# Queries' product ahead of the values' weights, and a last top-k search with keys and counts in PSUM

## The reference, cut to what matters

```python
def _L0_attn_ref(x, w_attn, b_attn, w_proj, b_proj):
    qkv = x @ w_attn + b_attn
    q, k, v = jnp.split(qkv, 3, axis=-1)
    mask = jnp.where(jnp.tril(jnp.ones((Tv, Tv), dtype=jnp.bool_)), 0.0, -10000000000.0)
    attn = jnp.einsum('btc,bsc->bts', q, k) / jnp.sqrt(jnp.float32(Cv)) + mask
    attn = jax.nn.softmax(attn, axis=-1)
    return jnp.einsum('bts,bsc->btc', attn, v) @ w_proj + b_proj

def _L0_ffn_ref(x, w_router, w_block):
    k = max(1, int(L * 0.75))
    _, top_idx = jax.lax.top_k(jnp.einsum('bld,d->bl', x, w_router), k)
    selected = jnp.take_along_axis(x, top_idx[:, :, None], axis=1)
    processed = jax.nn.gelu(jnp.einsum('bkd,de->bke', selected, w_block))
    return x.at[batch_idx, top_idx].set(processed)

x = layernorm(x + _L0_attn_ref(x, ...))
x = layernorm(x + _L0_ffn_ref(x, ...))
```

## Time and profile before

| | |
|---|---|
| device time, median of 3 executions | 1001.97 us |
| lowest, highest | 998.83, 1005.87 us |
| the profiled execution's own time | 998.7 us |
| its span | 997.0 us |
| granted clock, mean over the span | 0.975 |
| busy: PE, weight loads, DVE, ACT, POOL | 944.9, 804.5, 774.6, 634.8, 282.0 us |

### The profile page before, as it was taken

The page is one execution under the profiler, slowest core; times in us unless marked ns, Lnnn a source line. Parts: engine busy times, 40 slices in busy tenths (PEclk is TensorE's granted clock), DMA queues, the critical chain, the costliest instruction groups (busy, mean ns, idle before and its releaser), DMA issues.

```text
span 997.0 us, 15303 instructions
## 1 busy us (share of the span) xinstructions
PE 944.9 (95%) x4922; PEld 804.5 (81%) x4922; DVE 774.6 (78%) x1466; ACT 634.8 (64%) x1005; POOL 282.0 (28%) x433
## 2 busy tenths in 40 slices
PE   8899999999999999999999999999999999998960
PEld 6778888888888888888889888888878888886850
DVE  4585587968598597779778699888889869669777
ACT  2556476647485487459556476648579658439972
POOL 5251132222131115432233424232112212111441
PEclk8999999999999999999999999999999999999965
DMA  4643343434334335556733433534777544446815
GB/s 143 190 156 130 98 151 101 158 96 142 105 103 154 111 107 158 174 175 190 233 106 100 154 127 106 160 117 127 234 240 237 163 141 120 120 132 214 304 43 169
DMA packets 88947, 149.25 MB, mean 150 GB/s; under 512 B 7586, under 2 KB 25379, under 8 KB 88868
## 3 DMA queue, kind: packets, MB, share of 16 engines
q1 hardware_dynamic: 88868, 148.28, 46.9%
HBM read 108.40 MB, written 39.85 MB: 149 GB/s over the span
## 4 chain that ended last, share of the span: by engine, by line
PE 84%; DMA 6%; DVE 3%; ACT 3%; issue 2%; POOL 1%; SPq 1%; ACTq 0%; DVEq 0%; POOLq 0%
PE sbank L490 33%; PE fbank L490 12%; PE obank L932 11%; PE obank L934 11%; PE obank L933 11%; DMA xraw<-xt 2%; DMA tail<-y_scratch 2%; PE fbank L1009 1%; PE fbank L1109 1%; DMA out<-tail 1%; DVE tail L1426 1%; PE mbank L869 1%; PE mbank L848 1%; ACT parts L893 0%; ACT ring L773 0%
## 5 line engine op out<-in xcount | busy, mean ns | idle before, releaser
L490 PE MATMUL sbank<-qT,xT 128*128 128x512 f32 (+2 forms) x1728 | 409.6, 378 | 5.0 <-ACT qT L697 2.7
L490 PEld LDWEIGHTS sbank<-qT,xT 128*128 128x128 f32 x1728 | 305.2, 188 | 60.3 <-ACT ring L773 4.8
L773 ACT COPY ring<-sbank 128x512 f32<-128x512 f32 (+3 forms) x288 | 157.3, 549 | 144.1 <-PE sbank L490 106.3
L932 PE MATMUL obank<-ring_lo,vs 128*128 128x512 f32 (+3 forms) x576 | 217.9, 378 | 5.9 <-DVE ring_lo L898 3.2
L934 PE MATMUL obank<-parts,vs 128*128 128x512 f32 (+3 forms) x576 | 216.7, 376 | 0.0
L933 PE MATMUL obank<-parts,vs 128*128 128x512 f32 (+3 forms) x576 | 216.5, 376 | 0.0
L898 DVE TENSOR_TENSOR ring_lo<-ring,parts 128x1024 fp32r<-128x1024 f32 (+4 forms) x176 | 180.8, 1041 | 16.9 <-ACT parts L893 15.8
L879 DVE TENSOR_TENSOR ring<-ring,mbank 128x1024 f32<-128x1024 f32 (+4 forms) x176 | 159.7, 948 | 2.5 <-PE mbank L869 2.4
L893 ACT CAST parts<-ring 128x1024 fp32r<-128x1024 f32 (+4 forms) x176 | 144.7, 836 | 19.1 <-PE obank L934 18.5
L886 ACT ACTIVATE ring<-ring 128x1024 f32<-128x1024 f32 (+4 forms) x176 | 143.4, 844 | 19.6 <-DVE ring L879 19.1
L815 DVE TENSOR_TENSOR runmax<-ring,runmax 128x1024 f32<-128x1024 f32 x84 | 111.1, 1323 | 36.8 <-ACT ring L773 36.2
(11 more groups left out here) (172 smaller groups left out, 970.8 us busy)
## 6 DMA issues: line engine op xcount, KB each, us to landing
vs<-v_scratch SPq DMA_DIRECT2D x288, 256.0 KB, 2.8
v_scratch<-vnew SPq DMA_DIRECT2D x32, 512.0 KB, 3.1
xraw<-xt SPq DMA_DIRECT2D x16, 512.0 KB, 4.3
xres<-x SPq DMA_DIRECT2D x16, 512.0 KB, 3.9
out<-tail SPq DMA_DIRECT2D x32, 256.0 KB, 3.3
x_scratch<-xres SPq DMA_DIRECT2D x14, 512.0 KB, 3.0
y_scratch<-yb SPq DMA_DIRECT2D x14, 512.0 KB, 4.0
tail<-x_scratch SPq DMA_DIRECT2D x28, 256.0 KB, 3.4
```

The lines of the kernel that those rows point to most:

```text
L490: mm = eng.matmul(o, lhs(lh, k), rhs(rh, k), start=n == 0, stop=n == len(todo) - 1)
L773: act.copy(slot(n)[:, c0:], sbank[n % NSS][:, c0:]).then_inc(a_copy, 1)
L932: pe.matmul(o, vh, lo_, start=i == 0, stop=False)
```

## The change

It has five parts.

1. *The start.* On PE, `values_weights` becomes four operations of one matmul each and goes with `bias` into the stream "proj", right before the values' product of group 0, so behind the queries' product. On SP the first xᵀ load moves into the stream "prepare", between `load_qk` and `load_w`, with a semaphore of its own (`ld_xt0`); "prepare late" is gone.
2. *The planner.* Other numbers in `PREFER_US` and `MARGIN_US`, 15 and 8 entries in place of 13 and 8. A float32 matmul is rehearsed at 4 passes and not 8, and PE's operations that start before 21 us count 1.85-fold.
3. *The last search.* Keys, counts and the keys of the last four rounds of batch 1 lie in the PSUM bank `obank[0]`, columns 64, 96 and 32 on, free by then. Compares go in two pieces of 16 columns (240 elements), and the counting matmuls with them, two and two; the first compare, with its keys, in a piece of the first 24 columns, which can run before the last group's scores are made, and one of the last 8. Batch 0 keeps its tiles and single compares.
4. *Ties, both searches.* One scan over both counted rows (64 values), one addition and two combined steps take the place of ten steps; `above` is gone.
5. *Smaller.* The `ff` product of the last two groups is two operations for the planner; `final own` and `final sums` are one operation for each tile; the picks count on a semaphore of their own.

No matmul is added or taken away.

```diff
+COLD_US, COLD = 21.0, 1.85
+PREFER_US = {"final scale": 100, "attention_out stats": 60, "row_max reduce": 60, "project qhi": 60,
+MARGIN_US = {"attention_out router": 3, "final scale": 1.5, "out": 1, "final result": 1, "final_roots": 0.6,
-        passes = 8 if rhs.dtype == F32 else 1
+        passes = 4 if rhs.dtype == F32 else 1
-        time = r.time
+        time = r.time * (COLD if e == "pe" and when < COLD_US else 1.0)
...
             at("sp", "prepare", load_qk)
-            at("sp", "prepare late", load_w)
-            at("sp", "prepare late", load_block)
+            project_load(0)
+            at("sp", "prepare", load_w)
+            at("sp", "prepare", load_block)
...
-            def values_weights(pe):
+            def values_weights(pe, m, k):
                 pe.wait_ge(ld_w, 16 * 3)
-                for m in range(CC):
-                    for k in range(CC):
-                        mm = pe.matmul(w_psum[:, m], wv_t[:, k, m * P:(m + 1) * P], wp[:, k, :], start=k == 0,
-                                       stop=k == CC - 1)
-                mm.then_inc(p_w, 1)
+                pe.matmul(w_psum[:, m], wv_t[:, k, m * P:(m + 1) * P], wp[:, k, :], start=k == 0,
+                          stop=k == CC - 1).then_inc(p_w, 1)
-            for op in (values_weights, bias):
-                at("pe", "prepare late", op)
+            pe_fill["values weights"] = [lambda pe, m=m, k=k: values_weights(pe, m, k) for m in range(CC) for k in range(CC)] + [bias]
...
-            at("sp", "project load", load)
+                sp.dma_start(xraw[:, :, :], xt_rows[b][:, :, g * GQ:(g + 1) * GQ]).then_inc(ld_xt if G else ld_xt0, 16)
+            at("sp", "project load" if G else "prepare", load)
...
-                pe_fill[("ff", G, j)] = lambda pe, j=j: pe_f(pe, j)
+                    pe_fill[("ff", G, j)] = [lambda pe, j=j, t=t: pe_f(pe, j, (t,)) for t in range(2)]
...
+        PIECES = [[(0, NT)], [(0, NT // 2), (NT // 2, NT)]]
+        FIRST_PIECES = [[(0, NT)], [(0, NT - COUNTED), (NT - COUNTED, NT)]]
+        pieces_of = lambda b, c: FIRST_PIECES[b] if c == 0 else PIECES[b]
+
+
+
+        top_keys = [keyf[:, 0], obank[0][:, 64:64 + NT]]
+        deep_keys = [keyf[:, 3], obank[0][:, 96:96 + NT]]
+        counts = [cnt[:, 0, :], obank[0][:, 32:32 + RADIX]]
...
-                link(dve, dve.tensor_scalar(keyi[:, 0], bits, 31, -2147483648, ALU.arith_shift_right,
+            def make_keys(dve, lo, hi):
+                dve.wait_ge(v_sc, 2 * (b * NG + hi // QT))
+                if b:
+                    dve.wait_ge(v_cnt, 2 * ROUNDS)
+                    dve.wait_ge(v_top, 1)
+                bits, k = score[:, b, lo:hi].bitcast(I32), slice(lo, hi)
+            def top_count(dve):
+                dve.wait_ge(a_ot, CC * (len(groups) - 1) + 1)
+                dve.memset(counts[1][:, 0:1], float(T)).then_inc(v_top, 1)
-            def compare(dve, c):
-
+            def compare(dve, c, piece):
+                lo, hi = pieces_of(b, c)[piece]
                 if c == 0:
-                    make_keys(dve)
-                elif c == ROUNDS:
+                    make_keys(dve, lo, hi)
+                elif c == ROUNDS and not piece:
                     low_keys(dve)
-                keys = keyf[:, 0] if c < ROUNDS else keyf[:, 3]
-                dve.scalar_tensor_tensor(out=cmp[:, :, :], in0=keys[:, None, :].broadcast_to([P, RADIX - 1, NT]),
+                keys = (top_keys if c < ROUNDS else deep_keys)[b][:, lo:hi]
+                dve.scalar_tensor_tensor(out=cmp[:, :, lo:hi],
+                                         in0=keys[:, None, :].broadcast_to([P, RADIX - 1, hi - lo]),
                                          scalar=tab[:, c, 0:1],
-                                         in1=jtab[:, c, :, None].broadcast_to([P, RADIX - 1, NT]), op0=ALU.subtract,
-                                         op1=ALU.is_ge).then_inc(v_cmp, 1)
-                if c == 0:
+                                         in1=jtab[:, c, :, None].broadcast_to([P, RADIX - 1, hi - lo]),
+                                         op0=ALU.subtract, op1=ALU.is_ge).then_inc(v_cmp, 1)
+                if c == 0 and hi == NT:
                     lower_halves(dve)
...
+                dve.tensor_reduce(counts[b][:, 1:RADIX],
                                   bank_of(cnt_step[c])[:, 0:(RADIX - 1) * COUNTED].rearrange("p (j i) -> p j i",
                                                                                              j=RADIX - 1),
                                   AX.X, ALU.add).then_inc(v_cnt, 1)
                 dve.wait_ge(v_cnt, count_no(c) + 1)
                 after = {ROUNDS - 1: 2 * ROUNDS, 2 * ROUNDS - 1: 2 * ROUNDS + 1}.get(c, c + 1)
-                link(dve, dve.scalar_tensor_tensor(out=cnt[:, 1, :], in0=cnt[:, 0, :], scalar=float(TOPK),
+                link(dve, dve.scalar_tensor_tensor(out=cnt[:, 1, :], in0=counts[b], scalar=float(TOPK),
...
+                ahead = keyf[:, 0:2].rearrange("p s i -> p (s i)")
+                link(dve, dve.tensor_tensor_scan(ahead, ones[:, 0:2 * NT], tot, 0.0, ALU.mult, ALU.add))
+                dve.tensor_tensor(keyf[:, 2], ahead[:, NT - 1:2 * NT - 1], within, ALU.add).then_inc(v_tie, 1)
+                dve.wait_ge(v_tie, b + 1)
+                link(dve, dve.scalar_tensor_tensor(out=keyf[:, 0], in0=keyf[:, 2], scalar=float(TOPK), in1=gteq[:, 1],
+                                                   op0=ALU.is_lt, op1=ALU.mult))
+                link(dve, dve.scalar_tensor_tensor(out=left_out if b else sel[:, 1], in0=keyf[:, 0], scalar=0.0,
+                                                   in1=gteq[:, 0], op0=ALU.add, op1=ALU.is_equal))
+                if not b:
+                    link(dve, dve.tensor_scalar(sel[:, 0], sel[:, 1], -1.0, 1.0, ALU.mult, ALU.add))
+            if b:
+                at("dve", "search first", top_count)
             for c, step in enumerate(cnt_step):
-                at("dve", "search", lambda dve, c=c: compare(dve, c))
+                pieces = pieces_of(b, c)
+                counting = []
+                for piece in range(len(pieces)):
+                    def count(pe, c=c, step=step, piece=piece):
+                        lo, hi = pieces_of(b, c)[piece]
+                        pe.wait_ge(v_cmp, compared(c, piece))
+                        if not piece:
+                            freed(pe, step)
+                        o = bank_of(step)[:, 0:(RADIX - 1) * COUNTED].rearrange("p (j i) -> p j i", j=RADIX - 1)
+                        for i in range(lo, hi, COUNTED):
+                            mm = pe.matmul(o, ones_bf[:, :], cmp[:, :, i:i + COUNTED], start=i == 0,
+                                           stop=i + COUNTED == NT)
+                        if hi == NT:
+                            mm.then_inc(p_last if b else p_out, 1)
+                    counting.append(count)
                 at("dve", "search", lambda dve, c=c: decide(dve, c))
-
+                pe_fill[step] = counting
...
+            for t in range(2):
+                at("act", "final own", lambda act, t=t: own(act, t))
+                at("act", "final sums", lambda act, t=t: sums(act, t))
...
+                if f == ("v", 0, 0):
+                    for make in pe_fill["values weights"]:
+                        at("pe", name, make)
+                for make in pe_fill[f] if isinstance(pe_fill[f], list) else [pe_fill[f]]:
+                    at("pe", name, make)
```

130 lines of the change are left out of this document (56 added, 74 removed).

## The result

The changed kernel took 993.42 us in the median of 13 executions (990.39 to 997.15), the kernel before 1000.20 in 13 executions taken with them (997.34 to 1010.18). The ratio is 0.992 (95% interval 0.9893 to 0.9947); ratios here are taken over all executions and not from the two medians, whose quotient would be 0.993. Forecast were 995.5 us, 6.5 less than the median of 1001.97 shown. The profiled execution took 993.49 us, its span is 991.8. By its interval the gain lies between 0.5 and 1.1%: of the three cases of the prediction "within 1%" is the likely one, though a gain of just over 1% is not ruled out.

A forecast was written before the change was run, and what follows sets the result against it. PE's matmuls bound 100 to 890 us, so gains lay outside: start -2.1, to 100 us -0.8, last group -2.1, search -1.5, together -6.5 from 1001.97 to 995.5 us; own range 991.5 to 999.5, 8 in 10 within 988.5 to 1002.

The forecast's parts named there:

- within 1%: Whole kernel: measured time changes by no more than one per cent, 10 us, either way; chance 0.73.
- The term of the start: Start, up to the next group's score product: -2.1 us, ends -4.7 and +1, from an earlier queries' product.
- -0.8 between 40 and 100 us: PE's 2.9 us of idle time from 40 to 100 us: -0.8 us, ends 0 and -2.9.
- The middle: 0: Groups between start and last group, queues reordered by new planner's numbers: 0 us, ends -3.5 and +12.
- the fourth rival: Middle: score copies lose rank to ACT's casts, 12 us over 15 groups, so slower at 1007.5 us; chance 0.07.
- The last group -2.1: Turn to the last group: fifth unit 0.75 us sooner, a 1.36 us tile moved into the gap; ends 0 and -6.
- The search -1.5: Last search on DVE: three edits (PSUM keys and counts, two pieces, shorter selection) sum to -1.5 us, ends -3.5 and +1.
- the selection: End of the last search: ten dependent steps of 2.1 us become four taking 1.05, so -1.1 us.
- the pieces: Last search, compares in two pieces: nothing either way, within 0.1 us a round; early 24 columns +0.5 us.
- (a): Last search, keys and counts in PSUM: no stretched deciding steps, two being 1.9 us over medians; counted as -1.2 us.
- the first: Start: early lead eaten by a slow xraw load and late first score copy, 998.4 us; chance 0.17.
- the third: Last search: steps on PSUM operands 0.07 us dearer, costing 1.7 us, 997.2 us in all; chance 0.05.

The follow-up runs named there:

- old_search: Changed kernel with batch 1's search as before (keys and counts in SBUF, one piece, old ties); 997.09 us, ratio to before 0.9977.
- vlo_first: Changed kernel with the values' lo part and row constant of group 0 moved ahead of DVE's first mask addition and running maximum; 993.60 us, ratio to before 0.9944.
- start_only: Kernel before with only SP's and PE's new order of the preparation; old planner's numbers and searches; 1002.34 us, ratio 1.0010.
- planner_only: Kernel before with only the new planner's numbers; start streams and both searches as before; 995.04 us, ratio 0.9941.
- tail_only: Kernel before with only the new search for batch 1; start, planner's numbers and batch 0's search as before; 999.94 us, ratio 1.0005.
- keys_sbuf: Changed kernel with batch 1's keys and counts in SBUF again, order of every engine held; 998.88 us, ratio to before 0.9988.
- warm_chain: Changed kernel with idle PE matmuls in three places and all last-search key steps written to PSUM; 992.67 us, ratio to before 0.9897.
- weights_mid: Changed kernel with the four values' weights matmuls on PE between A's product and the bias sums; 994.82 us, ratio to before 0.9942.
- xor_psum: Changed kernel with the last search's first integer, an operand of the xor, in PSUM too; 995.12 us, ratio to before 0.9933.

## Why the prediction came out right, and where it was wrong

In the sum it was right: -6.5 us forecast; -6.8 between the medians, 0.992 as a ratio. In its terms it was not. The term of the start failed, the search was undersized, and the two errors met: that the sum came out so close is luck. By the ratios, all that precedes the search is worth 2.3 us (old_search, 0.9977, with an interval that reaches 1.0004) where the prediction has 5.0.

- *"A ready near 4.8, done near 8.5", the queries' product "4.7 us earlier, at about 10.8"*: 4.81, 8.37 and 11.39. Right; and it ran cold again, 4.57 us, as allowed for. *"First copy near 23.3"*: 23.39. Right.
- *"The row maxima of group 0 come no earlier, by my steps 0.7 us later"*, and *34.9 for the next score product, term -2.1*: wrong. I let the second values' half wait for a store "as before", and did not ask what the earlier third cast starts on POOL. It starts two subtractions beside which two DVE steps ahead of the store take 1.7 us longer, and it holds ACT's first values' cast back by 1.1; the store, the bank and PE follow: 39.68, 2.7 us later than before. Where all of it went is not shown, for vlo_first took the two steps out of the store's way and won nothing. That the moved start brings the wait by itself is shown by start_only (4.93 us, ratio 1.0010). The contended rows were in my own list of the last search; I looked for them only there.
- *"-0.8 between 40 and 100 us"*: the sign was right and the size too small. PE's idle time there went from 2.9 us to 0, and planner_only shows it for the new numbers alone (0.4). The one trace of before was also an early one. A second execution of the same queue reached the queries' product 6 us later, so the median could have had more to win than the trace showed; start_only, which had this to win too, won nothing.
- *"The middle: 0"*: 3.9 and 3.6 us of idle time. Right. But my ground against the fourth rival, that no wait for a score copy is over 0.8 us, was one execution's; tail_only, with the same queue, has one of 1.8.
- *"The last group -2.1"*: the two waits fell by 1.2 us, and in this pair of traces the half clock stayed. From the last row-max step on PE (the transposes of L869, now L874) to the landmark it takes 52.6 us instead of 51.7, with 228 matmuls instead of 222: the tile did move into the gap. Less its 1.36 us, that is 0.5 won. In the eight traces with this order and no half clock the stretch takes 50.9 to 52.0, which is 1.1 to 2.2 won against the trace of before. All four traces with the old order have the half clock there. So the term was about right at its upper end, and the pair of traces understates it.
- *"The search -1.5"*: 4.2 in the pair of traces, 2.1 to 3.4 by exchanging it. Of this the selection gave 2.91 to 1.82 us, the 1.1 forecast; the pieces 0 to 0.4. The mis-sized term is (a), put at -1.2: without operands in PSUM the search is 3.2 us longer (keys_sbuf). The trace of before already has a third stretched deciding step, 0.70 us at 972.56, which the prediction did not count; any step of the chain between SBUF and SBUF can stand still; and in keys_sbuf the delay of 0.8 us put the block's product on PE at the lower clock, 1.2 us more. The shares do not add up (old_search gives all of them back and is 3.4 us longer, not 4.3 or more): each is one trace. The reserve "the next counts queue behind the block products, so I count not all of it" pointed the wrong way for this.
- Not foreseen: the xor at 956.63 stands still too, 1.1 us; in the trace of before (957.26, 0.19 us) none of POOL's long additions lay beside it.
- Rivals: the first had the right outcome for the start (the lead eaten), but its sign, a late first score copy, did not come (23.39): of the store's 2.9 us ACT's wait for xraw has 1.1, through the values' cast, and the two DVE steps 1.7; the third is refuted; the fourth did not come.

## What to carry to other kernels

Before a transfer or a cast is asked for earlier, list what the engine behind it will then run beside, above all POOL beside DVE: here two DVE steps of 0.29 and 0.43 us took 0.99 and 1.40 beside POOL and held a store, and a lead of 4 us on PE was gone at the next group's scores. In a chain of short dependent DVE steps, an operand or a result in PSUM cost nothing here (464 against 465 ns) and took POOL out of it (no deciding step of 64 over 0.18 us), but each link has to be looked at, since the addition catches whichever link between SBUF and SBUF begins beside it. And a chain that hands over between engines gives a saved microsecond back wherever its next count is queued behind somebody else's wait.

## What the hardware showed that was not expected

- The time at which PE reaches the upper clock at the start differs between executions of one queue, with 6 us at the queries' product (15.45 and 21.50). Eight idle matmuls while PE waits for its first loads took half a per cent off the kernel before. With twenty in the wait that was 5.75 us long the clock stayed full from 15.4 to 950.6 us in one trace of warm_chain; in all nine other traces with the moved start it fell once between 28 and 34 us.
- A DVE step of 8 elements a partition from SBUF to SBUF, with one input, took 1.18 us beside POOL's addition (963.65), as a two-input one did (1.27); with its result in PSUM the same step took 0.17 beside it.
- The middle varies too: PE's idle time from 100 to 890 us runs from 2.5 us (weights_mid) to 6.5 (xor_psum) over nine executions whose queues there are the same.
